# Row transposes of the expert slots moved behind the down product, two slots ahead, with a second home for the transposed rows

## What is computed

```python
x = layernorm(x + attn(x))
logits = x @ router_w.T
top_vals, top_idx = top_k(logits, 1)
scores = sigmoid(logits at top_idx, -inf elsewhere)
xr = x[None] * scores.T[:, :, None]
gate, up = split(einsum('eth,ehf->etf', xr, gate_up_proj))      # 256 -> 2 * 512
routed = einsum('etf,efh->eth', up * silu(gate), down_proj).sum(0)  # 512 -> 256
shared = silu(x @ shared_gate_w) * (x @ shared_up_w) @ shared_down_w
x = layernorm(x + shared + routed)
```

## Time and profile before

| | |
|---|---|
| median of 3 runs | 549.71 us (549.06 to 550.59) |
| profiled execution | 548.86 us, span 547.0 us |
| PE busy | 534.8 us, 98% of the span |
| PEld busy | 451.7 us, 83% |
| DVE, POOL, ACT busy | 406.3, 337.2, 228.8 us |
| granted clock, 400 to 500 us | 1.00 |
| PE busy, 400 to 500 us | 100.00 us |

### The profile page before, as it was taken

The page is one execution under the profiler, slowest core; times in us unless marked ns, Lnnn a source line. Parts: engine busy times, 40 slices in busy tenths (PEclk is TensorE's granted clock), DMA queues, the critical chain, the costliest instruction groups (busy, mean ns, idle before and its releaser), DMA issues. The chain is left out here.

```text
span 547.0 us, 11800 instructions
## 1 busy us (share of the span) xinstructions
PE 534.8 (98%) x3830; PEld 451.7 (83%) x3830; DVE 406.3 (74%) x892; ACT 228.8 (42%) x410; POOL 337.2 (62%) x330
## 2 busy tenths in 40 slices
PE   8999999999999999999999999999999999999994
PEld 7777887887888888888787688888888888888884
DVE  5896987887887887887977687666866666666664
ACT  4445552553552552552443775233333333333331
POOL 1956676673783585774574577437776665555644
PEclk9999999999999999999999999999999999999998
DMA  8930508207606206304464904956677666655551
GB/s 263 322 106 3 192 3 175 96 1 192 195 1 192 80 2 165 106 0 155 156 233 150 371 21 155 330 148 193 191 173 203 192 197 202 190 178 183 194 183 40
DMA packets 46554, 83.82 MB, mean 153 GB/s; under 512 B 11360, under 2 KB 30576, under 8 KB 46480
## 3 DMA queue, kind: packets, MB, share of 16 engines
q1 hardware_dynamic: 38720, 64.52, 37.4%
q0 software_dynamic: 6112, 15.40, 10.2%
q10 hardware_dynamic: 1664, 3.15, 1.7%
HBM read 61.11 MB, written 22.34 MB: 153 GB/s over the span
## 5 line engine op out<-in xcount | busy, mean ns | idle before, releaser
L1751 PE MATMUL duo<-w_gu_hi,xsT 128*128 x320 | 107.2, 397 | 0.0
L1751 PE MATMUL duo<-x1T,wsgu 128*128 128x512 f32 x366 | 86.9, 392 | 0.4 <-DVE hT L1298 0.4
L1751 PEld LDWEIGHTS duo<-x1T,wsgu 128*128 128x128 f32 x366 | 68.1, 188 | 14.9 <-DVE hT L1298 0.8
L1162 POOL DMA_INDIRECT out_rows<-of,seat x39 | 39.4, 1011 | 56.7 <-DVE of L1708 55.0
L1751 PEld LDWEIGHTS duo<-w_gu_hi,xsT 128*128 128x128 f32 x320 | 59.7, 188 | 11.2
L1751 PE MATMUL duo<-w_gu,xsT 128*128 x160 | 62.0, 387 | 0.0
L1663 DVE SCALAR_TENSOR_TENSOR eh<-duo,seat,e_act 128x512 f32<-128x512 f32 x38 | 28.5, 751 | 39.9 <-PE duo L1751 39.9
L988 POOL TENSOR_TENSOR turned<-turned,swapped 128x1024 f32<-128x1024 f32 x16 | 38.4, 2401 | 29.1 <-DVE swapped L1226 29.1
L1235 DVE TENSOR_TENSOR sims<-duo,causal 128x512 f32<-128x512 f32 x64 | 41.0, 682 | 15.7 <-ACT sims L727 15.7
L1153 POOL DMA_INDIRECT xz<-xz_d,seat x39 | 45.5, 1166 | 8.9 <-issue 8.8
L727 ACT ACTIVATE sims<-duo 128x256 f32<-128x256 f32 x64 | 21.1, 381 | 64.3 <-PE duo L1831 64.0
(11 more groups left out here) (216 smaller groups left out, 1292.9 us busy)
## 6 DMA issues: line engine op xcount, KB each, us to landing
dn_rest<-dn_lo_d SPq DMA_DIRECT2D x39, 512.0 KB, 4.2
w_gu<-L_ffn_gate_up_proj SPq DMA_DIRECT2D x8, 1024.0 KB, 8.2
x_in<-x_t SPq DMA_DIRECT2D x8, 512.0 KB, 7.0
x_res<-L_attn_x SPq DMA_DIRECT2D x8, 512.0 KB, 4.0
dn_raw<-L_ffn_down_proj SPq DMA_DIRECT2D x8, 512.0 KB, 8.1
dn_hi_d<-dn_top SPq DMA_DIRECT2D x8, 512.0 KB, 4.5
dn_lo_d<-dn_low SPq DMA_DIRECT2D x8, 512.0 KB, 5.8
xz_d<-zs SPq DMA_DIRECT2D x8, 512.0 KB
```

What stands on the lines that cost most here:

```text
L1162: pool.indirect_dma_start(out, bass.IndirectOffsetOnAxis(ap=seat[:, s, 1:2], axis=0), of[:, s % OUTS, :], None).then_inc(sig.out_done[s % ...
L1751: last = mm(out_, left(a, k), right(b, k), start=start and k == 0 and n == 0, stop=stop and k == kt - 1 and n == len(PASSES) - 1)
```

## The change

PE now does in iteration s: gate and up of s, down of s-1, row transposes of s+2, transposes of `eh` of s. ACT and DVE copy the transposed rows of s+2 behind `ehT` and `ehT_lo` of s. Since rows of s+2 are copied while the product of s+1 has still to read its own, there are two homes: `xsT` for even slots, `xsT1` for odd ones. `xsT1` lies over the memory of `wsd`, so its first filling waits for the last shared down product. Row transposes of slots 0 and 1 stand before the loop, slot 1's behind the shared down product. The gathers are issued as before.

```diff
-        wsd = sb("wsd", [P, FT, D])
+        with ExitStack() as downs:
+            wsd = tensors(downs)("wsd", [P, FT, D])
+        xsT1 = sb("xsT1", [P, 2, KT, P], F32R)
+        past_xsT1 = sb("past_xsT1", [P, FT * D - 2 * KT * P])
...
+        def xs_of(s):
+            return xsT1 if s % 2 else xsT
...
             def rows_hi(s):
                 if is_slot(s):
                     act.wait_ge(sig.xsT_ps, at(s + 1))
-
-                    act.wait_ge(sig.eg_ps, at(2 * s))
-                    nc.scalar.activation(xsT[:, 0, :, :], duo[3][:, 0, 0:D].rearrange("p (k n) -> p k n", k=KT),
+                    if s == 1:
+                        act.wait_ge(sig.dn_ps, 2 * PAIRS)
+
+                    act.wait_ge(sig.eg_ps, at(2 * (s - 1)))
+                    nc.scalar.activation(xs_of(s)[:, 0, :, :], duo[3][:, 0, 0:D].rearrange("p (k n) -> p k n", k=KT),
...
             rows_hi(0)
+            rows_hi(1)
             for s in range(LAST):
...
-                rows_hi(s + 1)
                 act.wait_ge(sig.ehT_ps, s + 1)
...
                     .then_inc(sig.ehT_ok, 1)
+                rows_hi(s + 2)
...
             rows_lo(0)
             shared_sum(PAIRS - 1, 1)
+            rows_lo(1)
             for s in range(SLOTS + 2):
                 if s < LAST:
                     slot_act(s)
-                    rows_lo(s + 1)
...
                 if s < LAST:
                     hidden_lo(s)
+                    rows_lo(s + 2)
...
                     down_part(3, range(FT)).then_inc(sig.dn_ps, 1)
+                    if f == PAIRS - 1:
+                        slot_transposes(1)
...
                     slot_gate_up(s, this_e)
                     next_e = expert_of(s + 1)
-                    slot_transposes(s + 1)
...
                     slot_down(s - 1, last_e)
                 if s < LAST:
+                    slot_transposes(s + 2)
                     slot_hidden(s)
```

More of the change, by code:

```diff
@@ L1653, in rows_lo @@
                     dve.wait_ge(sig.xsT_hi, at(s + 1))
-                    nc.vector.tensor_tensor(xsT[:, 1, :, :], duo[3][:, 0, 0:D].rearrange("p (k n) -> p k n", k=KT),
-                                            f32(xsT[:, 0, :, :]), ALU.subtract).then_inc(sig.xsT_lo, 1)
+                    nc.vector.tensor_tensor(xs_of(s)[:, 1, :, :], duo[3][:, 0, 0:D].rearrange("p (k n) -> p k n", k=KT),
+                                            f32(xs_of(s)[:, 0, :, :]), ALU.subtract).then_inc(sig.xsT_lo, 1)
             def slot_act(s):
@@ L2223, in slot_gate_up @@
                 for half in range(2):
-                    three(duo[s % 2][:, half, :], lambda part, k: xsT[:, part, k, :],
+                    three(duo[s % 2][:, half, :], lambda part, k: xs_of(s)[:, part, k, :],
                           lambda part, k: gu_flat[part][:, bass.ds(e * (KT * 2 * FF) + (k * 2 + half) * FF, FF)],
@@ L2259, in last_gate_up @@
                     for half in range(2):
-                        three(last_gu(part)[:, half, cols], lambda n, k: xsT[:, n, k, :],
+                        three(last_gu(part)[:, half, cols], lambda n, k: xs_of(LAST)[:, n, k, :],
                               lambda n, k: gu_flat[n][:, bass.ds(e * (KT * 2 * FF) + (k * 2 + half) * FF + HALF_FF * part,
```

## The result

| | before | after |
|---|---|---|
| median of the runs | 549.55 us (549.06 to 550.59, 4 runs) | 569.96 us (569.57 to 571.87, 4 runs) |
| profiled execution: time / span | 548.86 / 547.0 us | 570.26 / 568.4 us |

The ratio is 1.038, 95% interval 1.0366 to 1.0394: 20.4 us slower. The forecast was 562.0, range 555 to 569. The sign was right and the size too small by 8 us, 1 us beyond the upper end of the range.

A forecast was written before the change was run, and what follows sets the result against it. PE, busy 98% of the span, was taken as the bound. Delays of 1.3 (head), 8.6 (slots 3 to 15) and 2.4 (slots 16 to 38) gave 12.3 on 548.86, 561.2, plus 0.85: 562.0 us, range 555 to 569.

The forecast's parts named there:

- Step 1: Row transposes moved on PE: 0.11 us each in either place, taken as 0, bounds 0 and 3.0 us gained.
- D: Delay of PE so far against the kernel before, summed over late gathers; forecast 12.3 us at the end.
- Step 2: PE asks for gathered rows 3.4 us earlier while gathers are issued as before; every us late costs a us.
- Step 3: The low row copy on DVE, now ahead of the norm, delays norm, scatter and next gather by 0.33 us.
- The sum, slots 15 to 38: Late gathers at slots 27, 36 and 38 cost 0.4, 1.1 and 0.9, together 2.4 us; median landing 4.2.
- rival (landings 5.5, 0.56 a slot): All gathers land slower, 5.5 us each, costing 13.4 us over 24 slots: 573 to 574 us; chance 0.06.
- The ring: PE and gathers wait on each other over two slots: 10.8 us against 9.72 at a landing of 5.5.
- waits in nearly every slot: Sign of a wrong forecast: PE waiting for gathers in nearly every slot, meaning landing or two-slot loop was mis-sized.
- Slots 3 to 15: PE delay from late gathers at slots 8 and 11 to 14, forecast 8.6 us.
- Head: Slot 1's row transposes wait for its gather before the first product: 1.3 us.
- The clock rival: The clock falls in PE's new pauses of 2.4 us: 572 us for two slots at the lower level; chance 0.03.
- The third rival: Gathers take 2.6 us, so only slots 1 and 8 are late: +2.1, 551.0 or 551.8 us; chance 0.02.

The follow-up runs named there:

- experiment 1: Changed kernel with POOL issuing gather s+4 at the start of iteration s, one slot earlier and ahead of the scatter: 551.38 us, ratio 1.0035.
- experiment 3: Changed kernel with the norm ahead of the low copy of the rows of s+2 on DVE: 562.76 us, ratio 1.0239.
- experiment 6: Kernel before with one extra small power operation on POOL ahead of each gather from slot 15 on: 549.67 us, ratio 1.0003.
- experiment 4: Changed kernel without the 512 KB loads of low down weights after the first three slots (old weights multiplied): 556.84 us, ratio 1.013.
- experiment 5: Kernel before with only slot 1's row transposes moved, ahead of the first gate and up product: 551.0 us, ratio 1.0024.
- experiment 10: Changed kernel with both the norm ahead of the low row copy and the 512 KB load waiting for the sum: 563.79 us, ratio 1.0272.
- experiment 2: Changed kernel with the 512 KB load of low down weights waiting for the sum on DVE, so later: 564.36 us, ratio 1.0304.

## Why the prediction was right in kind and wrong in size

**Step 1 holds.** In experiment 1, with the pairs in the new place, slots are 4.86 apart and D grows by 0.2 from slot 13 to slot 36. The place of the pair gives and costs nothing; the 3.0 us to be gained were not there.

**Step 2 holds.** The waits are where it put them: slot 1, slot 8, slot 11, slot 13, and some behind. Experiment 1 takes them away by issuing earlier. Two details were off. The transposes start 0.045 after the landing (I took 0.1), and a pair that waited takes 0.27 instead of 0.22, since its weight loads waited with it instead of running ahead.

**Step 3 holds in its size and not in its reach.** The norm starts 0.33 behind the start of the copy (488.35, 488.68). I counted that as 0.33 later gathers. It also moved each gather towards the load of `dn_rest`.

**The sum, slots 15 to 38, is the step that failed.** It says +2.4, with landings of 4.2 "of rows 9". Measured were 8.9 in the slots from 16 on. The term was mis-sized because the landing time of the kernel before was carried over as if it were a property of the gather. It was a property of the order of two transfers: 4.2 where the 512 KB load comes 1.08 behind the issue, 4.6 at 0.85 (experiment 3), 4.9 at 0.50 to 0.57 (the changed kernel, experiment 6), 3.5 where there is no load (experiment 4). It is not simply a matter of distance: at 0.0 it was 4.3 (experiment 1). With 4.2 a gather had 0.2 to spare; with 4.9 and without that 0.2 the forecast's own line reads 469.47 + 4.9 + 0.43 = 474.8 against 474.28, and nearly every pair waits. The prediction had priced this as a rival (landings 5.5, 0.56 a slot) at a chance of 0.06, because one of 23 took 5.5. By its own ring, 4.69 + 0.33 + 4.9 + 0.1 + 0.22 = 10.24 against 9.72, 0.26 a slot, 6 us over 23 slots, it would have given some 566 with the rest unchanged. Measured were 0.39 a slot. The ring can be added up from rows, gather by gather: a pair starts at its turn or 0.045 after the landing, and gather n+2 goes out 5.03 after the transposes of `eh` behind pair n (4.69 + 0.33). With a landing of 4.9 each this gives 6.3 us over the 23 slots. Gathers 23, 28 and 38, which POOL issues 0.4 to 0.5 later than that, add 0.9, and the landings as they were, some far above the median (up to 5.8), add 1.7: together 8.85, against 8.9 measured. With 4.2 each the same sum gives 0.8. So the ring was right and the landing time was the error, and in a ring a slow landing is not given back by a quick one. The prediction's own sign for this was "waits in nearly every slot (then the landing or the ring of two slots was mis-sized)".

The trace of before had a hint of it. Gathers 23, 28 and 38 went out there with the load 0.72, 0.58 and 0.62 behind them, and by the last updates of their semaphores they took 5.5, 5.0 and 4.8; the list of landings that I used leaves these three out. It was a hint and no proof: the longest landing of the list, gather 36 with 5.5, had the load 1.08 behind it like the others. I read the range 3.5 to 5.5 as scatter and did not ask what stood beside each gather.

**Slots 3 to 15:** 10.0 against 8.6. By their waits, slots 8 (1.55 against 2.4) and 11 (2.7 as forecast) were no worse than summed, slot 12 had none (1.1 forecast), slot 13 had 2.6 (1.8 forecast); small delays at slots 6, 7, 9 and 10 came to 1.6 (none forecast), and 1.5 was the clock, where 0.6 was forecast for slot 14. That the two sums for these slots are only 1.4 apart is in part luck.

**Head:** 1.9 against 1.3. Gather 1 landed in 8.45 us where it took 7.9 before; experiment 5 has 1.3 to 1.5 in its medians.

**The clock rival** was put at 0.03, as a fall in all long pauses. In the slots it fell once in the profiled execution, for 3.4 us and 1.5 us of time; the executions with a higher mean clock were 0.6 to 0.7 us quicker. The statement that the clock "falls only after PE has ended" was true of before alone.

**The third rival's rule** (only the head and slot 8 late, which did not come). By the Trainium skill, page "DMA: Bandwidth & Descriptors", section "Anatomy of one DMA", a DMA from GpSimd takes about 2.0 us plus its bytes over 436 GB/s, an estimate of 2.6 us for 256 KB. Even with the large loads taken away, the median was 3.5 and the least 3.3 (experiment 4). The measurement decides: here the rule is too low by 0.9 us without the load, and by 2.3 us with the load 0.5 behind.

## What to carry to other kernels

A landing time in a trace is the time of a transfer in its company: before you carry it over to a changed kernel, ask what else is issued within a microsecond of it, and whether the change moves that. When a consumer is moved earlier, move its producer by as much in the same edit; here one edit on POOL gave back 18 of 20 us. And look for a ring: where a late transfer delays the work that issues the next one, everything above the period is paid in every turn: here a landing 0.7 us longer and a copy of 0.33 us, both hidden in the order of before, became 9 us.

## What was not expected of the hardware

- An indirect gather of 256 KB, whose issue takes 1.07 us on POOL, is overtaken by a 512 KB load from another queue that is issued 0.5 us behind it. Counted from the gather's issue, the load then lands at 4.3 us and the gather at 4.9; before it was 5.25 and 4.2 (medians). The load's own time from issue to landing went from 4.2 to 3.8 in the changed kernel and in experiment 6.
- The granted clock fell to 1.2 GHz at waits of PE of 1.91 (experiment 5), 2.33 (experiment 10), 2.46 (the changed kernel), 2.65 (experiment 2) and 2.92 us (experiment 3), each time for 3.4 us and 1.3 to 1.7 us of time. The fall came 0.6 and 0.1 us before PE worked again (experiment 2, the changed kernel) or 0.1 to 0.6 us after (experiments 3, 5 and 10). It did not fall at a wait of 2.45 at slot 11 of the changed kernel, nor at 1.99 in experiment 2, 2.23 in experiment 3 and 2.05 in experiment 10. What decides it is open.
- In the kernel with the gathers earlier, slots are 4.85 and 4.89 long in turn: the gate and up product of odd slots, which reads the second home, takes 2.65 us from the start of its first matmul to that of its last, that of even slots 2.61. In before both took 2.62. The cause is open; it is worth 0.2 us of D.
